# Moving the second feed-forward bias and the last bias off TensorE, and loading the last pass's second group into another buffer

## The reference, cut to what matters

```
xn = layernorm(x)
gnn = for each edge: w * features(dst), summed by src, divided by the sum of w   (4 heads of 64)
mix = xn; for l in 0..3:
    mix = mix + linear_attention(layernorm(mix)) @ Wo[l] + bo[l]
    mix = mix + gelu(layernorm(mix) @ W1[l] + b1[l]) @ W2[l] + b2[l]
x1  = x + gnn + mix
out = x1 + slice_attention(layernorm(x1)) @ W_out + b_out
```

## Time and profile before

| | |
|---|---|
| time, median of 3 runs | 3549.72 us (3547.07 to 3549.95) |
| profiled execution: time, span | 3542.55 us, 3540.8 us |
| PE busy | 3280.0 us, 93% of the span |
| PEld busy | 2325.2 us, 66% |
| DVE busy | 2344.0 us, 66% |
| ACT busy | 1188.5 us, 34% |
| POOL busy | 1981.9 us, 56% |
| mean granted TensorE clock | 0.968 |

### The profile page before, as it was taken

One profiled execution on the slowest core, in us unless ns is written; L12 is line 12 of the kernel. 1 busy time (PEld: TensorE's weight loads), 2 busy tenths in 40 slices (PEclk: granted clock), 3 DMA queues, 4 the chain that ended last, 5 costly groups with the idle time before them and its releaser, 6 DMA issues.

```text
span 3540.8 us, 43968 instructions
## 1 busy us (share of the span) xinstructions
PE 3280.0 (93%) x13948; PEld 2325.2 (66%) x13948; DVE 2344.0 (66%) x6105; ACT 1188.5 (34%) x2126; POOL 1981.9 (56%) x1746
## 2 busy tenths in 40 slices
PE   6887899999989999989999989988999999989989
PEld 4565566666756666766766666666766666655666
DVE  7887878885444444453468777776776767759941
ACT  3343232333333333333324433343433434312220
POOL 3210007777777777777746777774777777600000
PEclk9998999999999999999999999999999999999999
DMA  3332112222322222232234555554555555412124
GB/s 114 105 99 87 32 45 43 43 49 38 75 52 45 46 49 49 43 85 42 48 107 134 148 141 143 137 149 147 154 161 150 159 142 168 130 52 87 67 108 152
DMA packets 226436, 338.52 MB, mean 96 GB/s; under 512 B 52502, under 2 KB 180009, under 8 KB 225956
## 3 DMA queue, kind: packets, MB, share of 16 engines
q0 software_dynamic: 67840, 119.33, 15.7%
q1 hardware_dynamic: 120452, 161.93, 14.1%
q10 hardware_dynamic: 37920, 54.45, 4.8%
HBM read 247.40 MB, written 87.29 MB: 95 GB/s over the span
## 4 chain that ended last, share of the span: by engine, by line
PE 61%; DVE 13%; POOL 13%; issue 5%; DMA 4%; ACT 2%; DVEq 0%; ACTq 0%
PE bank_v L1715 14%; PE bank_a L1700 14%; POOL arena L772 13%; PE bank_e L1757 5%; PE bank_a L1617 4%; PE bank_v L1645 3%; PE bank_v L1605 3%; PE bank_v L1688 3%; PE bank_a L1546 3%; PE bank_v L1776 3%; DMA arena<-gather_table,arena 3%; PE bank_v L1866 3%; PE bank_v L1788 2%; PE bank_a L1628 1%; DVE acc L1102 1%
## 5 line engine op out<-in xcount | busy, mean ns | idle before, releaser
L806 POOL DMA_INDIRECT edge_records<-acc x800 | 962.7, 1203 | 535.3 <-issue 535.3
L772 POOL DMA_INDIRECT arena<-gather_table,arena x880 | 943.9, 1073 | 356.5 <-issue 260.2
L1715 PE MATMUL bank_v<-W_sb,gT 128*125 128x256 f32 x3200 | 746.7, 385 | 0.0
L1700 PE MATMUL bank_a<-hT,W_sb 128*128 128x500 f32 (+1 forms) x1664 | 716.6, 579 | 17.2 <-ACT gT L832 8.6
L1715 PEld LDWEIGHTS bank_v<-W_sb,gT 128*125 128x125 f32 x3200 | 592.3, 190 | 106.3 <-issue 23.2
L1700 PEld LDWEIGHTS bank_a<-hT,W_sb 128*128 128x128 f32 x1664 | 319.4, 195 | 327.6 <-issue 301.3
L1757 PE MATMUL bank_e<-arena 128*125 128x260 f32 x1760 | 454.9, 403 | 0.0
L832 ACT ACTIVATE gT<-bank_a,cols 128x500 f32<-128x500 f32 (+1 forms) x416 | 272.3, 661 | 377.4 <-PE bank_a L1700 376.5
L1757 PEld LDWEIGHTS bank_e<-arena 128*125 128x125 f32 x1760 | 322.1, 193 | 46.7 <-issue 1.4
L832 ACT ACTIVATE hT<-bank_a,cols 128x500 f32<-128x500 f32 (+1 forms) x208 | 144.9, 747 | 489.5 <-PE bank_a L1546 460.4
L1158 DVE TENSOR_TENSOR arena<-arena 128x1024 f32<-128x1024 f32 x220 | 268.2, 1219 | 0.0
(11 more groups left out here) (286 smaller groups left out, 4342.4 us busy)
## 6 DMA issues: line engine op xcount, KB each, us to landing
residual<-xs SPq DMA_DIRECT2D x60, 500.0 KB
xs<-residual SPq DMA_DIRECT2D x60, 500.0 KB
arena<-edge_rows ACTq DMA_DIRECT2D x220, 125.0 KB
queries<-qT_out SPq DMA_DIRECT2D x48, 500.0 KB
qT_in<-queries ACTq DMA_DIRECT2D x39, 500.0 KB
arena<-gather_table,arena POOLq DMA_INDIRECT x880, 3.7
edge_records<-acc POOLq DMA_INDIRECT x800
slice_weights<-arena SPq DMA_DIRECT2D x12, 1000.0 KB, 5.0
```

What stands on the lines that cost most here:

```text
L772: e.indirect_dma_start(g_of(j)[:, i, :], None, table_d, bass.IndirectOffsetOnAxis(ap=node[:, TE * j + i:TE * j + i + 1].bitcast(I32), axis ...
L806: e.indirect_dma_start(rec_d, bass.IndirectOffsetOnAxis(ap=pos_i[:, f:f + 1], axis=0), r3[:, f, :], None).then_inc(d_rec, 16)
L1700: o = e.matmul(b[:, 0:n], W[:, k, f * P:(f + 1) * P], hv[:, k, 0:n], start=k == 0, stop=k == KC - 1)
L1715: o = e.matmul(b[0:R, i % 2 * D:(i % 2 + 1) * D], gv[:, f, i * R:(i + 1) * R], W2_sb[:, f * D:(f + 1) * D], start=False, stop=f == FB - 1 ...
```

## The change

For b2: the matmul at the head of each pair of tiles goes, and the first product of each tile starts the sum in the bank. DVE adds b2, which SP has loaded to all 125 partitions of a new tile `b2_rows` (once per layer, behind the load of W2), to the group's residual rows in SBUF, in a new stage `add_b2` at f = 4 of the group's `up` stages. For b_out: the same tile is loaded once more in `total` END, and GpSimd adds it to x1 in place, in the `join` stages, after the layer norm has read x1; DVE waits for all 13 before the first `output`. The parts of b2 and b_out are no longer made, so six small DMAs to DRAM and two from it go in the set-up.

For the last pass: group 1 of pass 5 goes to `ek`, which the layers no longer use by then, and SP loads it in `total` PRE - 1, after a wait for the last `attend` of group PRE. The planner's numbers: `down` 1.65 for 1.75, the factor of `edges_at` 1.56 for 1.55, `join` 0 at added - 13.0, which puts it behind `total` PRE and one `up`.

```diff
@@ feed_forward_up
+            if f == 4:
+                put(0.0, "add_b2", l, s)
@@ feed_forward_down
-            put(1.75, "down", l, s, i, h)
+            put(1.65, "down", l, s, i, h)
@@ planner
-    edges_at = sorted_part + 1.55 * EC
+    edges_at = sorted_part + 1.56 * EC
-    beside.append((added - 14.0, ("join", 0)))
+    beside.append((added - 13.0, ("join", 0)))
@@ buffers
-        B2 = BO + DEPTH * D
-        BOUT = B2 + DEPTH * D
-        NBIAS = BOUT + D
+        NBIAS = BO + DEPTH * D
+        b2_rows = sb("b2_rows", [R, D])
-        in_flat = ((bo, 0, KB), (b2, KB, KB), (b_out, 2 * KB, KC))
+        in_flat = ((bo, 0, KB),)
-        x_of = lambda p, s: xs[use(p, s) % 3]
+        x_of = lambda p, s: ek[0:R, :] if (p, s) == (DEPTH + 1, 1) else xs[use(p, s) % 3][:, :]
@@ SP
                     before = divmod(use(p, s) - 3, NGR)
-                    if before[0] <= DEPTH:
+                    if (p, s) == (DEPTH + 1, 1):
+                        e.wait_ge(v_done, attend_end(LAST, PRE))
+                    elif before[0] <= DEPTH:
                         e.wait_ge(*x_stored(*before))
                     else:
                         e.wait_ge(join_set, before[1] + 1)
+                        if before[1] == 1:
+                            e.wait_ge(*x_stored(DEPTH, PRE))
+            def load_b2(l):
+                of = b2[l] if l < DEPTH else b_out
+                e.dma_start(b2_rows[:, :], of.partition_broadcast(R)).then_inc(d_b2, 16)
-                    e.wait_ge(d_flatout, 16 * 9)
+                    e.wait_ge(d_flatout, 16 * 3)
@@ SP, x_t 4; h1 of END (behind W2); total
+                        load_b2(0)
+                        load_b2(l + 1)
+                    if s == END:
+                        load_b2(DEPTH)
-                    if s == PRE:
+                    if s == PRE - 1:
+                        e.wait_ge(*x_stored(DEPTH, 1))
                         load_x(DEPTH + 1, 1, x_d[DEPTH % 2])
@@ GpSimd
+                elif stage == "join":
+                    s, = at
+                    t0, nt = groups[s]
+                    x1 = accv[:, t0 * ROW:(t0 + nt) * ROW].rearrange("p (t n) -> p t n", n=ROW)[:, :, 0:D]
+                    if s == 0:
+                        e.wait_ge(d_b2, 16 * (DEPTH + 1))
+                    e.wait_ge(h1_set, nth(DEPTH, s))
+                    e.tensor_tensor(x1, x1, bc(b2_rows[:, :].unsqueeze(1), [R, nt, D]), ALU.add).then_inc(x1_set, 1)
@@ DVE
+                elif stage == "add_b2":
+                    l, s = at
+                    X = tiles_of(x_of(l + 1, s), s)
+                    if s == 0:
+                        e.wait_ge(d_b2, 16 * (l + 1))
+                    step(e.tensor_tensor(X, X, bc(b2_rows[:, :].unsqueeze(1), [R, tiles(s), D]), ALU.add))
@@ DVE, output
+                    if s == 0:
+                        e.wait_ge(x1_set, NGR)
@@ PE, down (output alike, with bias_rows(BOUT, D) and q for f)
-                        both = bias_rows(B2 + l * D, D).unsqueeze(1).to_broadcast([3, 2, D])
-                        e.matmul(b[0:R, :].rearrange("p (j n) -> p j n", j=2), ones3[:, 0:R], both, start=True, stop=False)
                         o = e.matmul(b[0:R, i % 2 * D:(i % 2 + 1) * D], gv[:, f, i * R:(i + 1) * R],
-                                     W2_sb[:, f * D:(f + 1) * D], start=False, stop=f == FB - 1 and i % 2 == 1)
+                                     W2_sb[:, f * D:(f + 1) * D], start=f == 0, stop=f == FB - 1)
```

## The result

The changed kernel takes 3520.38 us (median of 4 runs, 3516.72 to 3526.13) against 3549.10 for the kernel before (4 runs beside them, 3547.07 to 3549.95): a ratio of 0.9921, 95% interval 0.9904 to 0.9939, 28.7 us less. A second set of runs gave 3520.26 and again 0.9921 (0.9906 to 0.9937). The forecast was 3526, a gain of 23.5, with a range of 3508 to 3540. The profiled execution took 3516.72 us with a span of 3514.9, 25.9 us less than the span of before.

What follows compares the result with a forecast made beforehand. GpSimd's pace was taken to bound the kernel from 530 to 3088 us, PE and DVE before and after. Terms -13.8 - 1.7 - 14 + 9 + 2 + 1 - 6 = -23.5 us took 3549.7 to 3526, range 3508 to 3540.

Steps and rivals of the forecast that it cites:

- output, 25 biases: Output stage: 25 bias matmuls off PE at 0.55 us each, all of it kept, minus 13.8 us.
- three biases behind the last block: Three b2 bias matmuls on PE behind the last block count in full, minus 1.7 us.
- join and first slice groups: Last pass: the early load removes join 1's wait for store and load, PE's 11.1 us idle and slow start; minus 14 us.
- start of the gathers: First gather starts 2 us later (0 to 8), from adds on DVE while it still sorts.
- first blocks: Wait at the first blocks grows by 1 us, as acc memsets and five blocks stand where they stood.
- small waits for PE: GpSimd's 7 us of small waits for PE among the gathers go, minus 6 us.
- What bounds the kernel: GpSimd's pace of writes and gathers from 530 to 3088 us; PE and DVE set the time before and after.
- the 53 us: 97 biases before the last gather, booked as no gain; first rival: they arrive, 3467 us, chance 0.12.
- The adds on DVE: Each add holds GpSimd's DMAs 0.45 us (0 to 1.0): writes end 13 us later at cost 0, gathers plus 9 us.
- The adds on GpSimd: Thirteen b_out adds between slice groups, taken as 4 us each, inside 3.8 us of room plus 0.54 slack; cost 0.
- The second rival: GpSimd's add holds DVE's two-input op in 11 slice groups: loss 7 us at 5.0, 62 at 10 (3588); chance 0.10.
- Third and fourth rivals: Third: DVE adds cost GpSimd 1.0 us each, about 3550, chance 0.08. Fourth: early load doesn't help, 3540, chance 0.08.

Runs made afterwards that it cites:

- only_b2: Kernel before with only b2 moved to DVE, with the planner's new numbers: 3548.70 us, ratio 0.9997.
- only_bout: Kernel before with only b_out moved to GpSimd: 3531.30 us, ratio 0.9946.
- after_blocks40: Changed kernel with records, rows and first blocks due nearer to edges (14, 22, 38 us for 18, 30, 50): 3509.48 us, ratio 0.9901.
- before_half: Kernel before with two of a block's four gathers left out from block 6 on: 3449.39 us, ratio 0.9730.
- only_b2_oldplan: Kernel before with only b2 moved to DVE, with the planner's old numbers 1.75 and 1.55: 3538.46 us, ratio 0.9969.
- after_half: Changed kernel with two of a block's four gathers left out from block 6 on: 3381.85 us, ratio 0.9542 to the kernel before.
- after_pool3: Changed kernel with GpSimd adding b_out three times: 3526.21 us, ratio 0.9943 to the kernel before.
- after_no_add: Changed kernel with an empty add_b2, so b2 is never added: 3512.26 us, ratio 0.9905 to the kernel before.
- after_again: Changed kernel itself, run once more: 3520.26 us, ratio 0.9921 to the kernel before.
- only_ek: Kernel before with only the early load of group 1 into ek and its join 0: 3530.71 us, ratio 0.9949.
- after_oldplan: Changed kernel with the planner's old numbers 1.75 and 1.55: 3510.49 us, ratio 0.9912 to the kernel before.
- after_blocks30: Changed kernel with records, rows and first blocks due 10, 16 and 30 us behind edges: 3511.88 us, ratio 0.9906 to the kernel before.

## Why the prediction was right, point by point

The sum was -23.5, and the profile has -25.9, the medians -28.7. By its steps, with the rows of the changed kernel's one profile:

| step | forecast | measured |
|---|---|---|
| output, 25 biases | -13.8 | -14.7 |
| three biases behind the last block (measured: last gather to the last group's `up`) | -1.7 | -2.9 |
| join and first slice groups | -14 | -13.5 at the second group, -9.0 at the third |
| the rest of the slices and tokens | 0 | -1.9 |
| start of the gathers | +2 | +5.3 |
| first blocks | +1 | +9.9 |
| small waits for PE | -6 | -4.6 |
| weight parts, layer's turn | 0 | -6.8, -4.3 |
| adds and issue beside the gathers (measured: the remainder of the stretch) | +9 | +3.1 |

The measured terms behind the last gather come to -28.5 and those up to it to +2.6, against -29.5 and +6. The -2.9 is the distance from the start of the last gather to the start of the last group's `up` (3123.03 for 3123.37, so 33.3 us for 36.3). Only two of the three biases lie in it, 1.1 us; the rest is where the last gather falls against PE's work. The join terms are from there to line 1580 of the second group (24.9 for 38.4) and of the third (53.5 for 62.5). Of the -14.7 in the output, 13.5 are PE's and 1.2 the last store's.

- *What bounds the kernel* was right, and is shown: only_b2 gives nothing, and with half of the gathers 38 us of b2 come back. Of the 53 us the other 15 do not appear even then; what takes them is open.
- *The terms up to the last gather* met their sum by luck, +2.6 for +6. The start and the first blocks cost 12.2 us more than booked; the weight parts and the layer's turn, booked at 0, gave 11.1, the adds and issue came 5.9 below their term, and the small waits for PE gave 1.4 less than theirs.
- *The join*: the stall went whole. The prediction counted the slow start of one bank as gone with it, and in the changed kernel's two profiles three banks are slow behind the gap of 3.0 us (granted clock over the group 0.66 where it was 0.82), which gives 4.5 us back. This isn't the early load's price: only_bout has three slow banks without it, after_blocks40 one with it. The gap stands in all fourteen profiles, and the number of slow banks behind it varies: one in before, before_half, only_b2, only_b2_oldplan, after_half, after_blocks40 and after_pool3, two in after_no_add, three in after, after_again, only_ek, only_bout, after_oldplan and after_blocks30. With one, the third group starts 48.9 us behind `up` (after_blocks40), 13.6 less than before, so the -14 was right for that case. What decides between one and three isn't known.

```profile
3145.35 3.48 PE L1808 MATMUL bank_v<-Wqkv,hT 128*125 128x512 f32 x4 [3.01 <-ACT hT L857]
...
3149.11 1.98 PE L1808 MATMUL bank_v<-Wqkv,hT 128*125 128x512 f32 x4
```

- *The start and the first blocks* are where the working failed, though the sum hid it. It counted how late SP comes to `edges` and took the planner's two numbers for a shift that cancels. They move `records` on DVE and the first blocks as well. In the changed kernel the start is DVE's place in the list and not the writes' end: without the adds the writes end 11 us earlier and the first gather starts at the same time. By only_b2 against only_b2_oldplan the numbers cost 10 us, and by their medians after_blocks40 and after_oldplan have them back.
- *The adds on DVE* hold GpSimd as said, by 0.3 to 0.4 us each for the 0.45 forecast, beside the writes and beside the gathers. The writes' stretch grew by 13.4 us and 13 were forecast, but only some 8 of it are holds; the rest are the pauses of unknown cause, so this agreement is in part luck. The Trainium skill, "SBUF — State Buffer", section "Who interferes with whom", infers that such an operation doesn't hold descriptor generation, which gives 0. The gathers and writes held by the new adds, and the busy times with and without them, speak against it.
- *The adds on GpSimd* take 2.37 us, not 4, and cost nothing, as said. The estimate of 2.3 us from the Trainium skill's "GPSIMD Engine Reference", section "Elementwise — side-by-side cycle accounting", agrees. The second rival's rule is true and did not bite: the two engines do exclude each other, but for what is left of one instruction only. Its price of 11 x (T - 4.3) was for one long instruction, which no run has; three short ones of 7.1 us together lost a tenth to a fifth of it.
- *Third and fourth rivals*: the adds did not cost their bound; the early load helps by 11.9 us alone.

The medians of the single parts, -18.6, -18.0 and -0.6 us, come to 37, more than the -28.7 of all. The four intervals are 3.5 to 6 us wide on either side, so the difference of 8 us is not clear of them. Behind the last gather the parts are -11.9, -11.1 and -3.6, together -26.6 against -28.5, which agree within what the slow banks scatter (4.5 us). The last gather itself falls 6.5 us apart in the two profiles of the changed kernel (3089.7 and 3096.2). That these scatters explain the sum is argued, not shown.

## What to carry to other kernels

Before a saving is booked on the engine that looks full, ask which engine issues the work between here and there: a hundred matmuls gave nothing under GpSimd's chain of DMAs, and the 25 of the output gave all they had behind it. A planner's cost that is corrected moves everything placed by due time, and what was tuned at its edges (here `records` and the first blocks, 10 us) has to be placed anew; the fastest kernel here by its median is the changed one with these nearer to the load, at 0.9901. Before a few microseconds of one short stretch are put down to a change, look at the same stretch in the profiles of the other variants: the same gap was followed by one slow bank or by three, with the change and without it.

## What the runs showed of the hardware

- An operation of DVE with two SBUF inputs and GpSimd's add take turns by whole instructions: 2.29 us became 3.22, and 2.37 became 4.28 (after_pool3).
- An add of DVE with both inputs in SBUF holds an indirect DMA that GpSimd is issuing. In the kernel before, 178 of 880 gathers ended 0.81 to 0.83 us behind the end of a 1.22 us add, 0.53 us longer than the median on the mean.
- Behind a gap of 3.0 us on PE one to three banks of four matmuls ran at up to 3.78 us instead of 1.98, in all fourteen profiles. With three, the mean granted clock of the group was 0.66, so most of the time was at 1.2 GHz; over the 21 us behind the stall before, with two slow banks, it was 0.82.
- In the stretch of the gathers the mean granted clock was 0.97, with half the gathers 0.99. PE is idle for 95 to 132 us there with all gathers. In the 48 us before the output the clock was 0.89 after and 0.82 before; from the third slice group to the output PE was 1.9 us faster.
